# Sixteen turns written out, the position matrix added on TensorE, the expert choice made on logits, beta added to x once, features and gate split into row and token halves

## The reference, cut to what matters

```python
prod2 = einsum('bnt,btm->bnm', lhs2, rhs2)
S = einsum('kj,bij->bik', V_s, sigmoid(prod2 + b_s)); S = softmax(S, axis=1)
for k in range(3):
    r = einsum('mn,bmn,bmft->bnft', cheb[k], S, x)
    out = out + einsum('bnft,fo->bnot', r, Theta[k])
sg = relu(out);  tc = conv over t of sg with tw (width 3) + tb;  res = x @ rw + rb
y = relu(res + tc)
... layernorm over t:  (y - mu) / sqrt(var + 1e-5) * gamma + beta
x = x + that
... second block, on groupnorm(x), tokens of 256 channels:
logits = x @ gate_w.T;  probs = softmax(logits)
rw, sel = top_k(probs, 2);  rw = rw / sum(rw)
out += combine[:, e] * ((gelu(x @ w1[e].T) * (x @ w3[e].T)) @ w2[e].T)
x = x + out
```

## Time and profile before

| | us |
|---|---|
| median of 3 runs | 700.87 |
| the three runs | 702.01, 700.87, 695.55 |
| the profiled execution | 696.03 |
| its span, first to last instruction | 694.0 |

### The profile page before, as it was taken

One profiled execution on the slowest core, in us unless ns is written; L12 is line 12 of the kernel. 1 busy time (PEld: TensorE's weight loads), 2 busy tenths in 40 slices (PEclk: granted clock), 3 DMA queues, 4 the chain that ended last, 5 costly groups with the idle time before them and its releaser, 6 DMA issues. The chain is left out here.

```text
span 694.0 us, 12572 instructions
## 1 busy us (share of the span) xinstructions
PE 555.2 (80%) x2488; PEld 362.5 (52%) x2489; DVE 409.3 (59%) x1809; ACT 251.8 (36%) x619; POOL 213.7 (31%) x283
## 2 busy tenths in 40 slices
PE   0567599999999999999985225999999999999243
PEld 0233357766666666666663102666666666665122
DVE  4645236888888888988889771333333333332255
ACT  0343144345544444445442110333333333333232
POOL 5000001224333444443345440334334433443100
PEclk9989599999999999999999556999999999999655
DMA  9900000000000000000001032222222222221597
GB/s 299 421 4 1 0 1 1 0 1 32 31 30 30 31 30 30 30 23 23 27 27 55 31 106 70 77 85 83 84 85 91 78 85 87 91 83 42 164 321 240
DMA packets 36247, 52.69 MB, mean 76 GB/s; under 512 B 4606, under 2 KB 31361, under 8 KB 35969
## 3 DMA queue, kind: packets, MB, share of 16 engines
q1 hardware_dynamic: 24816, 30.86, 14.3%
q0 software_dynamic: 6480, 16.85, 6.5%
q10 hardware_dynamic: 4928, 4.72, 2.1%
HBM read 30.19 MB, written 23.14 MB: 77 GB/s over the span
## 5 line engine op out<-in xcount | busy, mean ns | idle before, releaser
L619 PE MATMUL bank<-w,xT 128*128 x284 | 135.9, 601 | 2.1 <-DVE xT L1420 2.1
L1420 DVE COPY xT<-bank 128x256 f32<-128x256 f32 x71 | 30.2, 425 | 143.8 <-PE bank L606 143.8
L975 POOL DMA_INDIRECT yrows<-xT,dest x71 | 69.4, 978 | 139.4 <-ACT xT L831 135.3
L496 PE MATMUL bank<-work 128*128 128x256 f32 x384 | 93.3, 386 | 0.0
L944 POOL DMA_INDIRECT xrows<-xtok,slot x64 | 64.3, 1005 | 81.4 <-DVEq L1315 66.7
L932 POOL TENSOR_TENSOR yg<-work,sml 128x512 f32<-128x512 f32 x16 | 18.0, 1122 | 196.3 <-DVE work L1225 193.0
L496 PEld LDWEIGHTS bank<-work 128*128 128x128 f32 x384 | 70.4, 190 | 9.0 <-issue 0.8
L634 PE MATMUL bank<-w,xT 128*128 x284 | 73.3, 380 | 1.6 <-ACT xT L836 1.6
L619 PEld LDWEIGHTS bank<-w,xT 128*128 128x128 f32 x284 | 48.8, 192 | 37.6 <-issue 37.6
L825 ACT ACTIVATE xT<-bank 128x256 f32<-128x256 f32 x71 | 27.4, 386 | 94.9 <-PE bank L619 94.9
L634 PEld LDWEIGHTS bank<-w,xT 128*128 128x128 f32 x284 | 48.5, 190 | 6.2 <-issue 2.6
(11 more groups left out here) (203 smaller groups left out, 1017.9 us busy)
## 6 DMA issues: line engine op xcount, KB each, us to landing
xT<-xrows SPq DMA_DIRECT2D x71, 129.0 KB
xT<-yrows SPq DMA_DIRECT2D x32, 256.0 KB, 3.9
xs<-x_in SPq DMA_DIRECT2D x4, 1024.0 KB, 10.8
w<-w13t_in SPq DMA_DIRECT2D x1, 4096.0 KB, 18.3
out<-xT ACTq DMA_DIRECT2D x16, 256.0 KB, 3.7
w<-w2t_in SPq DMA_DIRECT2D x1, 2048.0 KB, 22.7
yrows<-xT,dest POOLq DMA_INDIRECT x71, 2.4
xrows<-xtok,slot POOLq DMA_INDIRECT x64
```

Of the source, the lines that this page charges most:

```text
L496: last = mm(bank[6][:, h * N:(h + 1) * N], z[:, p, c, k, h], A[:, p, c, k], start=(c == 0 and k == 0), stop=(c == C - 1 and k == K - 1))
L619: last = mm(bank[2 + q][:, :], xc[:, q, c], w13[:, e, c].rearrange("p w n -> p (w n)"), start=(c == 0), stop=(c == C - 1))
L975: pool.indirect_dma_start(yrows, bass.IndirectOffsetOnAxis(ap=dest[:, q], axis=0), yo[:, q], None, bounds_check=2 * TOKENS - 1, oob_is_err ...
L1420: V.tensor_copy(xc[:, q].rearrange("p c k -> p (c k)"), bank[q][:, 0:C * P]).then_inc(c_xc, 1)
```

## The change

- `schedule` no longer makes a loop: all 21 turns are written out, with sample numbers known. `xTb`, `ghb` and the copies that fill them go; `mix`, `features` and `conv` read `xT` and `gh` themselves.
- `product` first multiplies the identity with `bs` into `bank[1]` and lets the old product add to it; `add_bs` goes, and `tanh` reads `bank[1]`. On ScalarE `tanh` now stands before `normalise`.
- `features` makes four matmuls of 64 rows and 192 columns for two of 128 rows and 384 columns. Rows 0 to 63 write one bank, rows 64 to 127 the other, and the zero blocks of `thetabd` are left out.
- The gate makes four matmuls of 128 tokens for two of 256; the token halves come out at partitions 0 and 64, and one transpose of 72 partitions takes the place of two of 8.
- The choice runs on logits less their maximum, 11 instructions in `route_b` (10 of them in a chain). The exponential is taken of one number per token, the second largest less the largest, and the weights are 1/(1+e) and e/(1+e), three instructions in `route_c`. `route_exp` moves behind `relu`.
- beta is added to all sixteen samples of `xs` by GpSimd ahead of the turns, and no more in `ln_out`.

```diff
-def schedule(eng, turn):
-    for i in range(-2, 4):
-        turn(i, i % 2, True, i + 1 >= 0, i >= 0, i >= 1, i >= 2, i >= 3)
-    with eng.Fori(0, (B - 6) // 2) as j:
-        for q in range(2):
-            turn(2 * j + (4 + q), q, *(True,) * 6)
-    for i in range(B - 2, B + 3):
-        turn(i, i % 2, False, i + 1 < B, i < B, i - 1 < B, i - 2 < B, True)
+def schedule(turn):
+    for i in range(-2, B + 3):
+        turn(i, i % 2, 0 <= i + 2 < B, 0 <= i + 1 < B, 0 <= i < B, 0 <= i - 1 < B, 0 <= i - 2 < B, 0 <= i - 3 < B)
...
-        pe.wait_ge(s["b_gb"], done(b))
         for h in range(H):
-            last = mm(bank[0][0:48, 0:N], ghb[:, p, h], xT[:, b, h], start=(h == 0), stop=(h == H - 1))
+            last = mm(bank[0][0:48, 0:N], gh[:, b, h], xT[:, b, h], start=(h == 0), stop=(h == H - 1))
...
     def product(b, p):
...
         for c in range(C):
+            mm(bank[1][:, c * N:(c + 1) * N], ident, bs[:, c], start=True, stop=False)
...
-                      lr[0:T, p, 0:N], start=True, stop=True)
+                      lr[0:T, p, 0:N], start=False, stop=True)
...
     def features(b, p, c):
-        pe.wait_ge(s["b_xb"], done(b))
+        pe.wait_ge(s["b_zc"], (b * 4 + c * 2) + START)
         for h in range(H):
-            pe.wait_ge(s["b_zc"], (b * 4 + (c * H + h)) + (START - 1))
-            mm(bank[4 + h][:, 0:K * P], xTb[:, p, h, c * P:(c + 1) * P],
-               thetabd[:].rearrange("p k t o -> p (k t o)"), start=True, stop=True).then_inc(s["b_z"], 1)
+            for r in range(2):
+                rows = slice(r * P // 2, (r + 1) * P // 2)
+                last = mm(bank[4 + r][:, h * K * P // 2:(h + 1) * K * P // 2], xT[rows, b, h, c * P:(c + 1) * P],
+                          thetabd[rows, :, r * TH // 2:(r + 1) * TH // 2].rearrange("p k t o -> p k (t o)"),
+                          start=True, stop=True)
+                if h == H - 1:
+                    last.then_inc(s["b_z"], 1)
...
     def tokens(b, p):
...
         for c in range(C):
-            last = mm(bank[3][0:E, 0:FT], sm("gate")[:, c * E:(c + 1) * E], xn2[:, c], start=(c == 0),
-                      stop=(c == C - 1))
+            for k in range(TT):
+                last = mm(bank[3][64 * k:64 * k + E, 0:P], sm("gate")[:, c * E:(c + 1) * E],
+                          xn2[:, c, k * P:(k + 1) * P], start=(c == 0), stop=(c == C - 1))
...
     def turn_logits(b, p):
...
-        for k in range(TT):
-            last = nc.tensor.transpose(bank[3][:, FT + k * E:FT + (k + 1) * E], lgT[0:E, k * P:(k + 1) * P],
-                                       cst[0:E, ID:ID + E])
-        last.then_inc(s["b_lg"], 1)
+        nc.tensor.transpose(bank[3][:, FT:FT + 64 + E], lgT[0:64 + E], cst[0:64 + E, ID:ID + 64 + E]
+                            ).then_inc(s["b_lg"], 1)
...
-    def fetch_xT(b, p):
-        act.wait_ge(s["b_conv"], done(b - 2))
-        nc.scalar.copy(xTb[:, p], xT[:, b]).then_inc(s["b_xb"], 1)
     def copy_tokens(b, p):
...
-        nc.scalar.copy(lgT[0:E], bank[3][0:E, 0:FT]).then_inc(s["b_gtc"], 1)
+        nc.scalar.copy(lgT[0:64 + E], bank[3][0:64 + E, 0:P]).then_inc(s["b_gtc"], 1)
...
     def tanh(b, p):
-        act.wait_ge(s["b_bs"], done(b))
-        nc.scalar.activation(sg[:, p], sg[:, p], ACT.Tanh, scale=0.5).then_inc(s["b_th"], 1)
+        act.wait_ge(s["b_pr"], done(b))
+        act.wait_ge(s["b_L"], done(b - 2))
+        nc.scalar.activation(sg[:, p].rearrange("p c n -> p (c n)"), bank[1][:, :], ACT.Tanh, scale=0.5).then_inc(s["b_th"], 1)
...
     def copy_features(b, p, c):
-        for h in range(H):
-            act.wait_ge(s["b_z"], (b * 4 + (c * H + h + 1)) + START)
-            nc.scalar.copy(z[:, p, c, :, h], bank[4 + h][:, 0:K * P].rearrange("p (k o) -> p k o", k=K)
+        for r in range(2):
+            act.wait_ge(s["b_z"], (b * 4 + (c * 2 + r + 1)) + START)
+            nc.scalar.copy(z[:, p, c, :, :, r * P // 2:(r + 1) * P // 2],
+                           bank[4 + r][:, 0:K * P].rearrange("p (h k o) -> p k h o", h=H, k=K)
...
     def route_exp(b, p):
-        act.wait_ge(s["b_sh"], done(b))
-        nc.scalar.activation(rt[:, 1], rt[:, 0], ACT.Exp).then_inc(s["b_ex"], 1)
+        act.wait_ge(s["b_df"], done(b))
+        nc.scalar.activation(r2[:, 9], r2[:, 4], ACT.Exp).then_inc(s["b_ex"], 1)
     def turn(i, q, ahead2, ahead1, now, back1, back2, back3):
-        if ahead1:
-            fetch_xT(i + 1, 1 - q)
...
-        if back3:
-            route_exp(i - 3, 1 - q)
...
+        if back3:
+            route_exp(i - 3, 1 - q)
...
+        if ahead2:
+            tanh(i + 2, q)
...
-        if ahead2:
-            tanh(i + 2, q)
...
-    schedule(act, turn)
+    schedule(turn)
...
+    over = lambda a: a.rearrange("p (u t) -> p u t", u=1).to_broadcast([P, C * 16, T])
+    flat = lambda a: a.rearrange("p c (o t) -> p (c o) t", t=T)
     def ln_out(b, p):
...
-        step = Steps(pool, p_x1, b, 2)
-        over = lambda a: a.rearrange("p (u t) -> p u t", u=1).to_broadcast([P, C * 16, T])
-        flat = lambda a: a.rearrange("p c (o t) -> p (c o) t", t=T)
+        step = Steps(pool, p_x1, b, 1)
...
-        step(nc.gpsimd.tensor_tensor(flat(yg[:]), flat(yg[:]), over(sm("beta")), ALU.add))
...
-    schedule(pool, turn)
+    pool.wait_ge(a_xna, B)
+    for b in range(B):
+        nc.gpsimd.tensor_tensor(flat(xs[:, b]), flat(xs[:, b]), over(sm("beta")), ALU.add).then_inc(p_beta, 1)
+    pool.wait_ge(p_beta, B)
+    schedule(turn)
...
-    def fetch_mix(b, p):
-        dve.wait_ge(s["b_gh"], done(b - 2))
-        V.tensor_copy(ghb[:, p], gh[:, b]).then_inc(s["b_gb"], 1)
-    def add_bs(b, p):
-        dve.wait_ge(s["b_pr"], done(b))
-        dve.wait_ge(s["b_L"], done(b - 2))
-        V.tensor_tensor(sg[:, p].rearrange("p c n -> p (c n)"), bank[1][:, :],
-                        bs[:].rearrange("p c n -> p (c n)"), ALU.add).then_inc(s["b_bs"], 1)
-        yield
...
-        lg = bank[3][:, FT:FT + TT * E].rearrange("p (k e) -> p k e", k=TT)
+        lg = bank[3][:, FT:FT + 64 * TT].rearrange("p (k e) -> p k e", k=TT)[:, :, 0:E]
...
     def route_b(b, p):
-        dve.wait_ge(s["b_ex"], done(b))
-        step = Steps(dve, v_rt2, b, 18)
-        yield from step.then(V.tensor_reduce(r2[:, 1], rt[:, 1], AX, ALU.add))
-        yield from step.then(V.reciprocal(r2[:, 2], r2[:, 1]))
-        yield from step.then(V.tensor_tensor(rt[:, 2], rt[:, 1], wide8(r2[:, 2]), ALU.mult))
-        src = rt[:, 2]
-        for w in range(2):
-            yield from step.then(V.tensor_reduce(r2[:, 3 + w], src, AX, ALU.max))
-            yield from step.then(V.tensor_tensor(rt[:, 3], src, wide8(r2[:, 3 + w]), ALU.is_equal))
-            yield from step.then(V.tensor_tensor(rt[:, 4], rt[:, 3], row8(cs(DSC, E)), ALU.mult))
-            yield from step.then(V.tensor_reduce(r2[:, 5 + w], rt[:, 4], AX, ALU.max))
-            yield from step.then(V.tensor_tensor(rt[:, 7 + w], rt[:, 4], wide8(r2[:, 5 + w]), ALU.is_equal))
-            if w == 0:
-                yield from step.then(V.scalar_tensor_tensor(out=rt[:, 5], in0=rt[:, 7], scalar=-2.0, in1=rt[:, 2],
-                                                            op0=ALU.mult, op1=ALU.add))
-                src = rt[:, 5]
+        step = Steps(dve, v_rt2, b, 10)
+        yield from step.then(V.scalar_tensor_tensor(out=rt[:, 4], in0=rt[:, 0], scalar=0.0, in1=row8(cs(DSC, E)),
+                                                    op0=ALU.is_equal, op1=ALU.mult))
+        yield from step.then(V.tensor_reduce(r2[:, 5], rt[:, 4], AX, ALU.max))
+        yield from step.then(V.tensor_tensor(rt[:, 7], rt[:, 4], wide8(r2[:, 5]), ALU.is_equal))
+        yield from step.then(V.scalar_tensor_tensor(out=rt[:, 5], in0=rt[:, 7], scalar=-3e38, in1=rt[:, 0],
+                                                    op0=ALU.mult, op1=ALU.add))
+        yield from step.then(V.tensor_reduce(r2[:, 4], rt[:, 5], AX, ALU.max))
+        dve.sem_inc(s["b_df"], 1)
+        V.tensor_scalar(xtok[:, p, :, N + 1], r2[:, 5], -1.0, float(E), ALU.mult, ALU.add)
+        yield from step.then(V.tensor_tensor(rt[:, 3], rt[:, 5], wide8(r2[:, 4]), ALU.is_equal))
+        yield from step.then(V.tensor_tensor(rt[:, 4], rt[:, 3], row8(cs(DSC, E)), ALU.mult))
+        yield from step.then(V.tensor_reduce(r2[:, 6], rt[:, 4], AX, ALU.max))
+        yield from step.then(V.tensor_tensor(rt[:, 8], rt[:, 4], wide8(r2[:, 6]), ALU.is_equal))
         yield from step.then(V.tensor_tensor(mb[:], rt[:, 7], rt[:, 8], ALU.add))
+        step.close()
...
-        V.tensor_scalar(xtok[:, p, :, N + 1], r2[:, 5], -1.0, float(E), ALU.mult, ALU.add)
-        yield from step.then(V.tensor_tensor(r2[:, 7], r2[:, 3], r2[:, 4], ALU.add))
-        yield from step.then(V.reciprocal(r2[:, 8], r2[:, 7]))
-        wb = wts[:, b]
-        V.tensor_tensor(wb[:, 0], r2[:, 3], r2[:, 8], ALU.mult)
-        yield from step.then(V.tensor_tensor(wb[:, 1], r2[:, 4], r2[:, 8], ALU.mult))
-        step.close()
     def route_c(b, p):
...
```

(8 more changed lines are left out.)

20 lines of the change are left out of this document (9 added, 11 removed).

## The result

The kernel before: median 697.57 us (695.22 to 702.01, 20 runs). The changed kernel: 702.95 us (696.92 to 705.53, 20 runs). The ratio is 1.0064, 95% interval 1.0044 to 1.0084: slower by 0.6%, inside the 1% that I had called the same, where I had forecast 684 and a range that ended at 701. The profiled execution after took 704.16 us with a span of 702.3, against 696.03 and 694.0.

A forecast was written before the change was run, and what follows sets the result against it. One ring through VectorE, ScalarE and TensorE bounds each turn, 18.44 to 17.56 us; ten turns -8.8, other turns -1.0 and -1.4, fill +2.0, drain -4.9 sum to -14.1; 14 below 698 gives 684 us, range 672 to 701.

The forecast's parts named there:

- The port: In the fill, GpSimd's beta additions can hold VectorE's small instructions, `nmx` among them: 0 to 2.2 us, taken as +1.0.
- The position matrix: In product on TensorE's arc, two added identity matmuls: 0.93 us plus 0.1 for shape switches, +1.03 a turn.
- my rival: Within the slower rival: changes of shape drain TensorE at 0.25 us each, eight a turn, giving 722 us.
- the other arc: VectorE and ScalarE from `prefix` to `turn_softmax`: 10.61 us before, forecast 9.60 without loop and copy.
- Features: On TensorE, split row halves run beside each other: a call falls from 1.38 to 0.93 us, -0.90 a turn.
- TensorE's arc: TensorE's part of a turn, from `turn_softmax` to the next `prefix`: 8.15 us before, forecast 7.96.
- The wait for `gr` goes: TensorE's 0.32 us wait in each steady turn disappears, as `gr` comes at 7.5 us behind `turn_softmax` or sooner.
- The gate: Between `prefix` and `turn_softmax` on TensorE, halves save some 0.35 us but give nothing in steady turns.
- Turn 13 to 14: The turn near the end with nothing ahead: forecast to gain 0.5 us.
- The drain: Turns 15 to the last slot: fewer choice instructions, port stalls gone and gate halves, -4.9 us in all.
- The slower one: In features every record's weight load is exposed, 2.9 us a call: 739 us; chance 0.10.
- The fourth: The ring is entered elsewhere, as by `nmx` held each turn, or code fetch stalls queues: 691 us; chance 0.10.

The follow-up runs named there:

- b1: The kernel before with beta alone moved to sixteen GpSimd additions ahead of the turns; 698.08 us (0.9960 to 1.0025).
- c6: The changed kernel with b_s added by VectorE again and the sixteen beta additions placed in VectorE's gaps ahead of the turns; 680.06 us.
- b4: The kernel before with its schedule alone written out, without the loop; 694.57 us (0.9918 to 0.9968).
- r2: b1's program run once more for one profile; 702.88 us.
- c1: The changed kernel with both b_s added by VectorE again and beta back in ln_out; 687.59 us (0.9786 to 0.9874).
- c3: a1 plus four identity matmuls, result unread, ahead of sample 0's softmax transposes; 695.62 us against the kernel before's 697.57.
- a1: The changed kernel with beta added per sample in ln_out again, without the row of sixteen additions; 699.63 us (0.9957 to 1.0026).
- b2: The kernel before with the position matrix alone: identity matmuls in product, no VectorE addition; 711.12 us (1.0131 to 1.0232).
- a5: The changed kernel with product reordered: one identity matmul of 512 columns first, then the two 16-row matmuls; 697.47 us (0.9972 to 1.0020).
- a4: The changed kernel with features whole again, matmuls of 128 rows and 384 columns; 708.55 us (1.0052 to 1.0156).
- a3: The changed kernel with b_s added by VectorE again and no identity matmuls; 687.52 us (0.9767 to 0.9827).
- d3: The changed kernel with each of the sixteen beta additions waiting until the one ahead has ended; 697.99 us (0.9926 to 1.0005).
- r1: The changed kernel run once more for one profile; 704.53 us.
- a2: The changed kernel with beta spread: six additions ahead, one at the head of each of turns 0 to 9; 704.92 us (1.0041 to 1.0105).
- e2: The changed kernel with beta as in c6 and the position matrix as one 512-column identity matmul ahead of turn_softmax; 676.27 us (0.9637 to 0.9719).

## Why the prediction was wrong, step by step

The sum was -14.1 us and the profiles show +8.1, 22 us apart. Ten of them lie in the fill, 5.5 in the ten turns, 3.1 in the turns at both ends (0 to 3, 13 to 15), 1.8 in the drain and 2 in stages without a changed line. In the prediction's own terms two steps failed: the port and what stands behind it in the fill, and the size of the position matrix.

**The port, +1.0 with bounds 0 and 2.2: failed.** I let a hold last as long as one GpSimd operation, since L1009 had ended with L932. That row had a free GpSimd behind it. In a row of sixteen, `nmx` was held through some four and a half of them. Bounds for a hold in a row are the row, 17 us. The Trainium skill (SBUF — State Buffer, the practical consequences of its ports) says that who comes second blocks until the first one's instruction is over. The 0.90 us of b1 agree with it, the 4.81 and 10.65 us do not: VectorE came second to the next instruction as well.

**What stands behind the wait: not in my list.** The prediction wrote of the lower clock only for the first turn, as something that ends by itself. The runs show that it comes again in or behind a wait. In the fill, with waits for `pn` of 0.4 to 1.6 us TensorE went on at the upper level; with 1.79 (c6) and 2.04 (b4) it fell 1.0 and 0.5 us behind the wait's end; with 2.3 and more the transposes themselves already ran at the lower one. The exception is r2, whose clock had fallen before, in a wait of 6.25 us for the copy. These are rows and no rule: the wait of 1.79 us from turn 13 to 14, below, came out both ways. So the delay of 38.75 - 26.52 = 12.2 us falls apart by c1 (26.22), c3 (28.65), a1 (34.78) and the changed kernel: the position matrix's own time 2.4, the clock 6.1, the hold 4.0, and 0.3 the other way. These sizes are differences of single profiles.

Why was the wait still 2.28 us in a1, with `nmx` free, where the kernel before has 1.57? From the end of `logits` to `pn` it is 3.3 and 3.2 us, and `mix` stands in between. In both the clock rose 11.2 us behind the first `mix`. But the second `mix` began 10.0 us behind the first before, and 11.5 in a1, with the longer `product` (4.6 us) ahead of it. So it ran at the upper level, in 1.06 us and not in 1.69, and what it saved became wait: part of the cost comes from being faster for half a microsecond. Luck has a hand in this. b2 makes the same matmuls as a1 up to this point, but there the clock rose only 14.1 us behind the first `mix`, so `mix` took 1.94 us and the wait was 1.32; in b4, with the work of the kernel before, it rose after 10.3, `mix` took 1.21 and the wait was 2.04. What sets that moment, the runs do not show. Nor do they show what ends the lower level: in b4 it lasted from 90.9 to 94.3 us, in a1 from 92.2 to 105.8, with TensorE busy 12.50 of 12.50 us from 93.0 to 105.5.

**The position matrix, +1.03: mis-sized, +1.45 measured.** Columns were right (a5: 1.05 for 512), and the missing 0.4 is the alternation, which I had put at 0.05 a change and a5 shows at 0.2. The earlier trace rows could not bound it, as `product` there changes shape once going in and once going out, and I took the difference of two modelled ends. a4 and a5 show a cost of 0.1 to 0.2 us at a change of shape, less than the 0.25 of my rival. The Trainium skill (TensorEngine Tiling (Array Packing), Key Properties) has TensorE drain when the mode changes. The two runs agree with it as to the place of the cost; that it is a drain they cannot show. I had set it aside too early.

Ten turns of 0.42 are 4.2 of the 5.5 us; the remaining 1.3 are 0.04 a turn on the other arc and three turns of 18.3 us among those of 18.03. In these three VectorE stood idle for about 0.2 us with nothing to wait for (issue), just ahead of the numbers that `gn_var` needs, and TensorE went from its transposes to `graph` in 0.9 us and not in 0.64:

```profile
215.50 0.18 DVE L1269 TENSOR_TENSOR rt<-rt,r 128x16 f32<-128x16 f32 x1 [0.23 <-issue]
```

Idle marked as issue was on my list of signs. It is there, and it cost 0.9 us in ten turns; whether fetching code is behind it no run shows. In the turns 0 to 2, which TensorE bounds alone, my +0.1 each became +0.77: without the matrix (a3, c1) they took 13.57 and 14.01 us, with it 15.01 and 15.46, so it cost 1.44 a turn there, too.

**Features, -0.90: right.** 0.85 a call for 1.38, where I took 0.93, so the halves do run beside each other; the stretches around them took 0.17 back. TensorE's arc shows it: without the wait for `gr` it was 7.83 us, with 1.45 for the matrix it would be 9.28, and it is 8.39, so 0.89 came off. (Undone in a4 it is worth 0.57, as a whole call takes 1.29 us there, ahead of the 128 rows that the matrix put into `product`.) **The other arc, 9.60: right**, 9.64, and piece by piece: `centre` was idle 0.23 us where I had 0.39 less 0.16, and L1248, the former L1263, 0.23 where I had 0.62 less 0.42. **The wait for `gr` goes: right**, 1.5 us to spare. **The gate:** TensorE waits 1.04 us for `pn` behind it, so what it saves is worth nothing in the steady turns, as said. Neither the gate nor the choice on logits was undone in a run of its own.

**Turn 13 to 14, -0.5: failed.** No `mix` stands ahead of the transposes, TensorE waited 1.79 us at 360.79, and the six records of `graph` behind it took 2.26 us for 1.54. The 0.7 us of this are luck, as a1 has the same wait without the fall, and so have a4, a5 and d3, while r1, c3 and a2 have it with the fall:

```profile
356.43 0.66 PE L471 MATMUL bank<-cst,pn 128*128 128x128 f32 x4 [1.79 <-ACT pn L748]
...
357.07 1.54 PE L493 MATMUL bank<-work 128*128 128x256 f32 x6
```

Without the fall the turn took 18.02 us in a1, which is still no gain on 18.07. Turn 14 to 15 gave 0.54 us of the 1.4; the other profiles with beta ahead and the matrix in `product` have it at 13.9 to 14.5 us, and why it gave less stays open.

**The drain, -4.9: right to 0.7** up to the last slot: ten steps, `mb` 2.05 us behind L1260 where before it took 15 steps. Behind it GpSimd's last scatter waited 2.59 us for the one before to land, a wait that the kernel before does not have, and began 1.80 us behind the slot for 1.04: a step made sooner met a transfer that had not moved. The 1.07 us of the table are not shown to come from it, as r1 has a wait of 2.57 and 13.07 us to the first expert.

Of the rivals, none had it. The slower one put the loss into the weight loads of `features`, which are hidden: a call takes 0.85 us, not 2.9. The fourth named `nmx` held by GpSimd, but in each turn; it was held in the fill, once. That the outcome lies so near to no change is luck: 12 us lost in the fill against 3 gained in the turns 3 to 13 and 4 in the drain.

## What to carry to other kernels

A wait costs more than its length if TensorE falls back to its lower clock in or behind it. Whether it does can be luck, so give a longer wait in a stage that is just coming up to speed two prices: its own length, and what follows until the clock is back (b4, whose work in the fill is that of the kernel before, paid 1.6 us for a wait of 2.04 where that one waited 1.57). Then see whether useful work of the same engine can stand in it (e2). Move work into idle time of an engine only after asking who shares a port with it there; and leave a seam between operations that go in a row (d3, one profile). Work on a bottleneck ring is priced by its place: the same identity matmul cost 1.45 us a turn in `product`, 1.05 as one block, and 0.5 in front of a wait.

## What the runs showed that I had not expected

- A two-column VectorE operation beside a row of overlapping GpSimd operations was held for 4.56 to 6.14 us in five profiles and a copy of 96 columns for 10.65 in another, each to the end of the row. Four other instructions were let in at a seam, after 0.89 to 1.07 us. With each operation waiting for the one before, it was 0.52.
- Taking the hardware loop of two turns away, and nothing else, gave 0.57 us a turn (b4).
- A change between 128-row and 16-row matmuls took 0.2 us, one between 128 and 64 rows about 0.1.
- Four matmuls whose result nobody reads made the fill 6.1 us shorter (c3).
- The same wait of 1.79 us was followed by a fall of the clock in four profiles and not in four others, and in two turns of c1 the clock fell though TensorE had waited no longer than in the turns beside them.
